# A planned kernel (Mamba block, experts, attention, MLP): other lengths and delays in the program that writes its instruction order

## The reference, cut to what matters

```python
xn = layernorm(x)
x = x + mamba_mlp_norm(xn) + experts(xn)              # layer 0
xn = layernorm(x)
x = x + attention_and_memory(xn) + lora_mlp(xn)       # layer 1

# mamba, per sequence: 512 channels, 16 states, a recurrence over 1024 tokens
h = exp(delta_t * A) * h + delta_t * B_t * u_t ;  y_t = sum over states of h * C_t
# then y * silu(res), output projection, MLP 256-1024-256 with exact gelu, a norm over the whole sequence
# experts, as written, come to a dense MLP 256-2048-256 on sequence 0, weighted per token
# layer 1: causal attention with 16 heads of 16 features, a memory gate built from 6-component lines,
# and an MLP 256-1024-256 whose weights get a rank-one-like correction per sequence
```

## Time and profile before

| what | us |
|---|---|
| median of the runs (3, from 3900.2 to 3905.79) | 3903.46 |
| the profiled execution, time on the device | 3907.57 |
| its span in the profile | 3905.8 |
| PE busy | 3610.2 |
| DVE busy | 3178.4 |
| ACT busy | 2659.1 |
| POOL busy | 2288.1 |

### The profile page before, as it was taken

How to read it: one execution, slowest core, us unless ns; L and a number is a source line. 1 busy time by engine, 2 the same in 40 slices (tenths; PEclk the granted TensorE clock), 3 DMA queues, 4 the chain that set the end, 5 groups by cost and what they waited for, 6 DMA issues and landing times.

```text
span 3905.8 us, 63544 instructions
## 1 busy us (share of the span) xinstructions
PE 3610.2 (92%) x20512; PEld 2387.7 (61%) x20512; DVE 3178.4 (81%) x6108; ACT 2659.1 (68%) x4049; POOL 2288.1 (59%) x1788
## 2 busy tenths in 40 slices
PE   7999999999999999999798999999999998999998
PEld 3666566655556565656565666666566666656665
DVE  3788999998999999998957687786868778686874
ACT  6877878787787878877534657566575656657565
POOL 4687898898999899999814142332414233241421
PEclk9999999999999999999897999999999999999999
DMA  4345444454544555554522123232322323232220
GB/s 155 126 155 162 154 156 157 161 165 151 163 161 153 159 164 171 162 166 144 184 74 90 52 58 97 72 100 67 99 65 69 93 68 104 67 94 64 73 80 26
DMA packets 253340, 456.88 MB, mean 117 GB/s; under 512 B 26116, under 2 KB 80852, under 8 KB 250196
## 3 DMA queue, kind: packets, MB, share of 16 engines
q1 hardware_dynamic: 253012, 452.82, 37.1%
HBM read 381.07 MB, written 69.21 MB: 115 GB/s over the span
## 4 chain that ended last, share of the span: by engine, by line
PE 46%; DVE 13%; ACT 9%; issue 8%; POOL 1%; DVEq 0%; ACTq 0%; POOLq 0%
PE ps L1495 6%; PE ps L1608 5%; PE ps L1600 5%; PE ps L1476 4%; PE ps L1458 3%; DVE ps L2013 3%; PE ps L1360 3%; PE ps L1410 2%; PE ps L1529 2%; PE ps L1370 2%; DVE ps L2036 2%; ACT L1625 2%; PE ps L1535 2%; ACT h L1625 2%; ACT exps L1625 2%
## 5 line engine op out<-in xcount | busy, mean ns | idle before, releaser
L2270 POOL TENSOR_TENSOR drive<-du,b_wide 128x1024 f32<-128x1024 f32 x512 | 1202.0, 2363 | 204.3 <-DVE held L2013 122.1
L2304 POOL TENSOR_SCALAR_AFFINE_SELECT exps<-exps 128x256 f32<-128x256 f32 x512 | 204.1, 413 | 1000.5 <-ACT exps L1625 1000.0
L1625 ACT ACTIVATE ps<-delta,neg_a 128x512 f32<-128x512 f32 x1024 | 681.7, 685 | 146.2 <-DVE heavy L1991 132.2
L1625 ACT ACTIVATE exps<-ps 128x1024 f32<-128x1024 f32 (+1 forms) x640 | 596.5, 938 | 255.2 <-PE ps L1476 249.2
L2036 DVE CUSTOM_DVE_ANT_0 ps<-ps,later 128x512 f32<-128x512 f32 (+3 forms) x1024 | 474.7, 518 | 90.6 <-PE ps L1458 88.6
L1410 PEld LDWEIGHTS ps<-p_all,heavy 128*128 128x128 f32 x3072 | 361.9, 144 | 246.5 <-DVE heavy L1991 124.8
L1410 PE MATMUL ps<-p_all,heavy 128*128 128x128 f32 x3072 | 439.9, 280 | 76.2 <-DVE heavy L1991 69.2
L1991 DVE TENSOR_TENSOR heavy<-c_wide,ps 128x512 f32<-128x512 f32 x704 | 467.6, 670 | 8.2 <-issue 4.1
L2013 DVE TENSOR_TENSOR_SCAN ps<-ps,carry,drive 128x512 f32<-128x512 f32 x352 | 441.5, 1272 | 32.8 <-ACT ps L1625 32.5
L2013 DVE TENSOR_TENSOR_SCAN ps<-ps,drive 128x512 f32<-128x512 f32 x352 | 420.4, 1214 | 48.3 <-ACT ps L1625 46.0
L2039 DVE TENSOR_REDUCE smax<-ps 128x2 f32<-128x1024 f32 x256 | 312.1, 1220 | 112.0 <-PE ps L1458 109.3
(11 more groups left out here) (211 smaller groups left out, 7158.7 us busy)
## 6 DMA issues: line engine op xcount, KB each, us to landing
b_wide<-bc_dram SPq DMA_DIRECT2D x512, 256.0 KB, 3.4
c_wide<-bc_dram SPq DMA_DIRECT2D x512, 256.0 KB, 3.5
stacks<-parts SPq DMA_DIRECT2D x192, 256.0 KB, 2.5
qs<-stacks SPq DMA_DIRECT2D x128, 192.0 KB
ks<-stacks SPq DMA_DIRECT2D x128, 192.0 KB, 4.3
x_row<-in_x SPq DMA_DIRECT2D x14, 1024.0 KB, 7.9
resid<-mix SPq DMA_DIRECT2D x9, 1024.0 KB, 5.3
x_row<-resid SPq DMA_DIRECT2D x9, 1024.0 KB, 5.4
```

What stands on the lines that cost most here:

```text
L1625: return nc.scalar.activation(out_, in_, func, **kw)
L2270: G.tensor_tensor(drive[:, g % DRIVE_SLOTS, :, :], du[:, e, :, :], wide(b_wide[:, g % B_SLOTS, :], MD), ALU.mult).then_inc(driven, 1)
```

## The change

It replaces the numbers in the planner's tables and adds three things to `by_time()`: a delay per producing engine (`LATE`) in place of 0.06 us for all, a delay between two dependent tasks of different kinds on the same engine (`OWN`), and an added 0.09 us from a scan to POOL. The share with which a PE task counts for the modelled clock is given per unit (`active_of`). `LEAD0`, `LEAD`, `LAG`, `SPANS`, `DRIFT`, `TURN`, `SHORT`, `RUN` and the ticks stay. One instruction of the fixed part moves: ACT's square root of the second part of sequence 0's layernorm now stands in the prelude, behind the drain of the second `xt` unit, and the first `norm` task is planned with 0.49 us in place of 3.2.

```diff
+LATE = {"p": 0.2, "a": 0.18, "v": 0.16, "g": 0.12, "s": 0.06}
+TO_POOL = 0.09
+OWN = {"p": 0.0, "a": 0.13, "v": 0.13, "g": 0.04}
-LENGTH0 = {"xt": 0.46, "xm": 1.74, "cv": 3.46, "res": 1.74, "xd": 3.46, "dl": 0.88, "yt": 0.46, "m": 3.46, "h": 1.74,
-           "o": 4.0, "mu": 0.4, "var": 0.4, "mh": 1.74, "mo": 3.5}
-EMPTY0 = {"xt": 0.66, "xm": 0.66, "cv": 0.66, "res": 0.66, "xd": 0.6, "dl": 0.68, "yt": 0.62, "m": 0.62, "h": 0.66,
-          "o": 0.42, "mu": 0.4, "var": 0.2, "mh": 0.62, "mo": 0.45}
+LENGTH0 = {"xt": 0.44, "xm": 1.72, "cv": 3.44, "res": 1.72, "xd": 3.46, "dl": 1.05, "yt": 0.44, "m": 3.46, "h": 1.72,
+           "o": 3.68, "mu": 0.2, "var": 0.2, "mh": 1.72, "mo": 3.46}
+EMPTY0 = {"xt": 0.48, "xm": 0.49, "cv": 0.58, "res": 0.49, "xd": 0.48, "dl": 0.59, "yt": 0.48, "m": 0.48, "h": 0.58,
+          "o": 0.33, "mu": 0.14, "var": 0.1, "mh": 0.49, "mo": 0.38}
...
-                add("v", ("scan", k), 1.2 if j % NC else 1.13, k, ("a", "decay", k), ("g", "drive", g),
+                add("v", ("scan", k), 1.175 if j % NC else 1.13, k, ("a", "decay", k), ("g", "drive", g),
...
-                    add("v", ("weigh", k), 0.6, k + 1.5, ("v", "scan", k), ("s", "c", g),
+                    add("v", ("weigh", k), 0.59, k + 1.5, ("v", "scan", k), ("s", "c", g),
...
-        add("v", ("gate", q), 1.66, at + NS * MD + 0.7, ("p", "add", piece_of(j, e + 1, 0, 0) - 1),
+        add("v", ("gate", q), 1.32, at + NS * MD + 0.7, ("p", "add", piece_of(j, e + 1, 0, 0) - 1),
...
-        add("a", ("norm", 0, t), 0.42 if t > TC else 3.2, t - TC - 2)
+        add("a", ("norm", 0, t), 0.49, t - TC - 2)
...
-            add("a", ("silu_x", j), 4.5, start + 2, ("a",) + unit)
+            add("a", ("silu_x", j), 4.4, start + 2, ("a",) + unit)
...
-            add("a", ("gelu", j), 6.2, start + 2, ("a",) + unit)
+            add("a", ("gelu", j), 6.1, start + 2, ("a",) + unit)
...
-LENGTH = {"xt": 0.44, "qk": 1.30, "pa": 1.18, "pb": 1.30, "lt": 0.44, "jw": 0.89, "fw": 0.44, "fr": 0.44, "ms": 0.44,
-          "zt": 0.44, "wo": 1.72, "e1": 0.23, "e2": 0.23, "f1": 1.30, "o": 3.44}
+LENGTH = {"xt": 0.44, "qk": 1.40, "pa": 1.28, "pb": 1.40, "lt": 0.44, "jw": 0.89, "fw": 0.44, "fr": 0.44, "ms": 0.44,
+          "zt": 0.44, "wo": 1.72, "e1": 0.23, "e2": 0.23, "f1": 1.46, "o": 3.44}
...
-    return 0.02 + sum(max(0.107, width_of(*one) / 2400) for one in unit)
+    return sum(max(0.12, width_of(*one) / 2230) for one in unit)
...
-WINDOW, LOW = 3.413, 0.45
-SHARES = {"sm": 0.5, "st": 0.5, "ms": 0.15, "e1": 0.03, "e2": 0.03, "mt": 0.25, "dl": 0.5}
+WINDOW, LOW = 3.413, 0.44
+ACTIVE0 = {"add": 1.2, "held": 1.2, "xt": 1.2, "yt": 1.2, "dl": 0.5, "mu": 0.0, "var": 0.0}
...
-        used[window] = used.get(window, 0.0) + part * share
+        used[window] = used.get(window, 0.0) + part * pace * active
...
                 for bank in banks[unit]:
-                    bank_free[bank] = end + 0.06
+                    bank_free[bank] = end + LATE[e]
...
-            felt = end + (late if one[0] != e or e == "s" else 0.0)
+            felt = end + (late if one[0] != e or e == "s" else OWN[e] if kind_of(one) != kind_of(name) else 0.0)
+            felt += TO_POOL if name[:2] == ("v", "scan") and one[0] == "g" else 0.0
...
                 elif kind == "norm":
-                    if (j, task[2]) == (0, TC):
-                        task_of(("root", 0, 1))
                     norm_tile(j, task[2])
...
                 if unit == ("cv", 0, MI - 1):
                     task_of(("silu_x", 0))
+                elif unit == ("xt", 0, 0, KD - 1):
+                    task_of(("root", 0, 1))
```

More of the change, by code:

```diff
@@ L219, in layer0_tasks, with add @@
     tasks, before = {}, {}
-    def add(engine, unit, length, tick, *after, late=0.06):
+    def add(engine, unit, length, tick, *after, late=None):
         kind = (engine, unit[0])
-        tasks[(engine,) + unit] = (length, tick, [a for a in after + (before.get(kind),) if a], late)
+        tasks[(engine,) + unit] = (length, tick, [a for a in after + (before.get(kind),) if a],
+                                    LATE[engine] if late is None else late)
         before[kind] = (engine,) + unit
@@ L502, in pair @@
             add("p", ("sm", g, n), scores_length(unit, max_width), tick, ("s", "stack", g) if n == 0 else None)
-            add("v", ("sm", g, n), sum(1.16 if it // TC > ch else 0.22 + max_width(it, ch) / 485 for it, ch in unit)
-                + (0.09 if n == len(MAX_UNITS) - 1 else 0), tick, ("p", "sm", g, n))
+            add("v", ("sm", g, n), sum(1.135 if it // TC > ch else 0.21 + max_width(it, ch) / 485 for it, ch in unit)
+                + (0.26 if n == len(MAX_UNITS) - 1 else 0), tick, ("p", "sm", g, n))
         place["mt", g] = first + TICKS - LEAD
@@ L554, in layer1_tasks @@
         for i in range(2):
-            add("s", ("rows", b, i), 3.8, start - 8, ("v", "split", b), ("p", "e2", b - 1, 3) if b else None,
+            add("s", ("rows", b, i), 3.3, start - 8, ("v", "split", b), ("p", "e2", b - 1, 3) if b else None,
                 late=3.0)
@@ L586, in layer1_tasks @@
             for ch in range(1, FCH):
-                add("g", ("sum", b, c, ch), 1.27, place["fr", b, c, ch] + 1, ("v", "fr", b, c, ch))
+                add("g", ("sum", b, c, ch), 1.22, place["fr", b, c, ch] + 1, ("v", "fr", b, c, ch))
             for i in range(2):
@@ L590, in layer1_tasks @@
             add("a", ("logistic", b, c), 0.5, place["ms", b, c, 1], ("v", "ms", b, c, 1))
-            add("v", ("gate", b, c), 2.9, place["ms", b, c, 1], ("a", "logistic", b, c), ("v", "pb", b, TC * c + TC - 1))
+            add("v", ("gate", b, c), 3.2, place["ms", b, c, 1], ("a", "logistic", b, c), ("v", "pb", b, TC * c + TC - 1))
         for kind in ("e1", "e2"):
@@ L612, in layer1_tasks @@
             dense(("wo", b, i), ("a", "zt", b, i // 2, KD - 1), v=[("v", "o", b, i, TQ - 1)])
-            add("s", ("store", b, i), 0.6, place["wo", b, i], ("v", "wo", b, i), late=3.0)
+            add("s", ("store", b, i), 0.5, place["wo", b, i], ("v", "wo", b, i), late=4.0)
     for g in range(PAIRS):
@@ L616, in layer1_tasks, with active_of, at_pace @@
     return tasks
-WINDOW, LOW = 3.413, 0.45
-SHARES = {"sm": 0.5, "st": 0.5, "ms": 0.15, "e1": 0.03, "e2": 0.03, "mt": 0.25, "dl": 0.5}
-def at_pace(used, start, length, share):
+WINDOW, LOW = 3.413, 0.44
+ACTIVE0 = {"add": 1.2, "held": 1.2, "xt": 1.2, "yt": 1.2, "dl": 0.5, "mu": 0.0, "var": 0.0}
+ACTIVE = {"xt": 1.2, "zt": 1.2, "lt": 1.1, "fw": 1.1, "fr": 1.1, "ot": 1.2, "mt": 1.2, "jw": 0.72, "ms": 0.24, "e1": 0.03, "e2": 0.03,
+          "pb": 0.62, "f1": 0.92}
+def active_of(unit, length):
+    if unit[0] != "L1":
+        return ACTIVE0.get(unit[0], 1.0)
+    if unit[1] in ("sm", "st"):
+        wide = places(MAX_UNITS[unit[3]], max_width) if unit[1] == "sm" else places(EXP_UNITS[unit[3]], exp_width)
+        return 1.1 * wide[1] / 2400 / length
+    if unit[1] == "pv":
+        return 2.56 * sum(exp_width(t, OUT_UNITS[unit[3]][1]) for t in OUT_UNITS[unit[3]][0]) / 2400 / length
+    return ACTIVE.get(unit[1], 1.0)
+def at_pace(used, start, length, active):
     now = start
@@ L703, in by_time @@
             mode = mode_of(unit)
-            end = at_pace(used, start, length, SHARES.get(unit[1] if unit[0] == "L1" else unit[0], 1.0))
+            end = at_pace(used, start, length, active_of(unit, length))
         del open_tasks[e][name]
```

96 lines of the change are left out of this document (49 added, 47 removed).

## The result

The changed kernel takes 3934.71 us (median of 4 runs, 3928.55 to 3936.72), the kernel before beside it 3903.88 (4 runs): **ratio 1.0077, 95% interval 1.006 to 1.0095**. It is 31 us slower, where 3883 was forecast with a range from 3845 to 3915. The profiled execution has a span of 3935.0 us. All lines of the program stand 25 lower in the file: L2013 is now L2038, L1458 is L1483, L1625 is L1650.

A forecast was written before the change was run, and what follows sets the result against it. It took PE as the bound to 330 us, DVE to 1962 and PE from 2140 to 3797. Terms of minus 9, 5, 0 and 6 made minus 20 us: 3883 us against a median of 3903.46, range 3845 to 3915.

The forecast's parts named there:

- The start, minus 9: Prelude: moving ACT's square root lets DVE and PE begin earlier, worth 9 us less.
- The 1.87 us of clock: Start: extra time of PE's next four matmuls at the lower clock, counted as gain beside 10.00 us of PE idle time.
- The lower of the two bounds: Start: DVE's own gain, its first scan at 58.5 instead of 61.30 us, 2.8 us; the upper end was 11.9 us.
- Lengths in layer 0, minus 5: Recurrence: more exact hand-off delays at 65 waits, 0.1 us each, taken as 5 us less; bounds minus 46 and plus 32.
- The hand-over, zero: The 178 us between layer 0 and layer 1: no change taken, bounds minus 10 and plus 10 us.
- Lengths in layer 1, minus 6: Layer 1: truer PE lengths and delays let other units fill part of PE's short waits, 6 us less.
- The bound on the bad side, plus 30: Layer 1: worst case for the term of minus 6 us, a good third of PE's 93.3 us idle time.
- The sign named for layer 1, a busy share of 94 to 95%: Layer 1: PE's busy share expected in the changed kernel's profile if the forecast holds.
- The other sign that it named, layer 1 alone moving by over 15 us: Layer 1: a move of over 15 us there would show the forecast to be wrong.
- (4): Slower: ACT's lumps in the recurrence come before decays and lose 32 to 48 us; 3926 us or more, chance 0.18.
- (2): Large gain, 45 to 65 us: half of DVE's 86 us of recurrence waits for ACT or POOL goes; 3851, chance 0.12.
- (3): No change: lists nearly alike, a small layer-1 loss takes back the start's 9 us; 3903 within 7.8 us, chance 0.15.

The follow-up runs named there:

- e1: The kernel before with only ACT's second square root moved into the prelude, all lists and banks unchanged: 3897.8 us, ratio 0.9985 to the kernel before.
- e2: The changed kernel, but with layer-1 task order and banks taken from the kernel before: 3894.6 us, ratio 0.9973 to the kernel before.
- e4: The changed kernel with the planner's modelled clock windows shifted by 1.7 us when layer 1's order is made: 3923.7 us, ratio 1.0056.
- e15: The changed kernel with layer 1's span `late` ending at 7 instead of 5 and modelled clock windows shifted by 1.7 us: 3890.5 us, ratio 0.9966.
- e3: Layer-0 order and banks of the kernel before, layer-1 order and banks of the changed kernel, square root moved: 3942.3 us, ratio 1.0106.
- e6: The changed kernel's layer 0; layer-1 lists from before's numbers with DVE drain `fr` at 0.76 instead of 0.75 us: 3934.4 us, ratio 1.0073.
- e5: The changed kernel's layer 0; layer-1 lists from before's numbers with modelled clock windows shifted by 1.7 us: 3932.5 us, ratio 1.0064.
- e11: The changed kernel with PE's old layer-1 lengths and LEAD, DRIFT, SHORT and span `mlp` reset, the planner's best of 320 settings: 3875.2 us, ratio 0.9923.
- e13: As e12, with the planner's modelled clock windows shifted by 1.7 us before the layer-1 lists are made: 3909.6 us, ratio 1.0014.
- e7: The changed kernel; layer-1 lists from the change's numbers with DVE drain `fr` at 0.68 instead of 0.67 us: 3931.1 us, ratio 1.0066.
- e14: As e12, with DVE drain `fr` planned at 0.68 instead of 0.67 us for the layer-1 lists: 3892.9 us, ratio 0.9961.
- e12: The changed kernel with layer 1's order made from the change's numbers but PE's lengths of before: 3884.6 us, ratio 0.9946.

## Why the prediction was wrong, by its own steps

**The start, minus 9.** The mechanism is right in its main steps: the root at 14.90 (forecast 14.9), DVE on at 15.13, the first scan at 59.32 (58.5). The size was too big. PE's idle time fell by 7.45 us, not 10, because ACT's drains of `delta` hold PE until 53.60 us, where the prediction has its list begin at 51.5. The 1.87 us of clock were hardly won back (3.55 against 3.75 us): the term assumed that a short gap leaves the clock up. It also read the clock wrong, which did not fall "while PE stood" but at 48.9 us, before PE stood; that gave 1.23 us at the end of the prelude which the term does not have. Alone the move is worth 4.8 us at 330 us and 5.9 (2.3 to 9.4) on the whole time (e1), and with the new lists of layer 0 only 1.9 are left at 330 us. The lower of the two bounds was nearer than I took it.

**Lengths in layer 0, minus 5.** With the start it was to be minus 14 at the last `gate`; it is minus 12.6. That agreement says little. The root alone gives 13.5 there, and 14 kernels with the very same lists of layer 0 (after, e2, e4 to e15) have that end between 1943.8 and 1956.0, mean 1949.4; the two with before's lists have 1948.0 and 1958.2. A term of 5 us can't be seen in this. It can be seen on the way: at the 512th scan, near 1030 us, the new lists are ahead of before's by 6.0 to 13.9 us, e1 and e3 with the root alone by 4.4 and 4.9. Little of the difference is left at the end of the layer.

**The hand-over, zero.** The cuts of 179 us above are of equal length because I set them so, and show nothing. Marks in the work do: counted from the last `gate`, the first score matmul starts at 38.0 us (before 46.6), the 48th matmul with the values at 120.3 (125.3) and the 384th, an eighth of them, at 350.3 (351.3). So zero is right to within a few us, and the loss lies behind these marks.

**Lengths in layer 1, minus 6.** This is the step that failed. It reads: "93.3 us of idle time at 0.51 us a wait are some 180 waits; if each gave 0.1 us, it would be 18 us. I take a third". It measured plus 42. The idle time was seen rightly as many short waits, and these did get shorter, by 16 us in the stretch. But the step treated a list as something that a better number improves a little everywhere. The list is rebuilt: another unit comes first, the rest follows, and 14 waits more than before are over 1 us. e2 and e3 put the whole loss on this list, and e6 shows that a change of no meaning costs as much. The bound on the bad side, plus 30, was worked out from idle time alone ("a good third of the idle time"). It left out that the instructions get longer too, which took as much again: 21 us idle and 21 us of longer instructions, with 75 us more at the lower level. The sign named for layer 1, a busy share of 94 to 95%, hides this: it was 93.4%, because the busy time grew as well. The other sign that it named, layer 1 alone moving by over 15 us, did show it.

**The rivals.** (4), slower, had the sign and nearly the time (3926 or more) but the wrong place: it put the loss in the recurrence, where waits for decays fell from 86.1 to 76.9 us. (2) fell: those waits were not halved. (3) said that ties depend on hundredths of a us, and used it only against "no change"; e6 shows that it is the main fact here. It should have widened the range: two redraws of before's own numbers lie 38 and 40 us above the list in place (e5, e6 against e2), and a range that ends at 3915 has no room for that. The chance of slower, 0.18, took the list in place for an average one.

**What stays open.** Which of the other numbers (delays, drains, DMA entries) alone helps or hurts in layer 1 was not tried one by one, and neither were order and banks. Why before's list was better than two redraws of it is not shown, though the planner's own model ranks it first. e11 was not redrawn, so it is a good list, not a proof of good numbers; e13 suggests that a redraw can cost 25 us.

## What to carry to other kernels

Where a program builds its order by playing numbers forward, any edit of a number draws a new list, right or not: here 0.01 us in one entry cost 1% of the time once (e6), and moved it by 0.1 and 0.2% in two other cases (e7, e14). So measure two or three trivial redraws before a change of numbers is judged, look first at the end that the model itself gives them, pick leads and spans again after it, and keep the fastest list by measurement.

To judge a list for a full PE by its profile, take the sum of all its idle time in the stretch. Over these 17 kernels the length of the stretch follows it with a correlation of 0.95 (a part of that is by construction, since the stretch is idle and busy time together), the number of gaps with 0.43, the sum of gaps over 1 us with 0.81 and the time at the lower level with 0.82. By the last two alone e5 (22 gaps in 39.3 us, 81.2 us at the lower level) and e12 (23 in 37.6, 81.6) are alike, and e5 is 48 us slower: its idle time is 115.8 us and e12's 90.7. The changed kernel had fewer waits than before and nearly the same busy share.

## What the hardware showed that I had not expected

- Idle time of PE in layer 1 comes with more than its own length. The gap before 3051.79 us (3.80 us idle) was followed by `f1` matmuls of 0.41 us against 0.28, and behind the last `gate` the 21 us of extra idle time came with 75 us more at the lower level and 21 us more busy time. Over the 17 kernels the stretch grows by 1.7 us for each us of idle time in it; that is a fit, and e5 against e2 has only 1.3 (14.9 us more idle time, 19.3 us longer, the same time at the lower level). At the start the four matmuls behind 2.55 us of idle time were nearly as slow as those behind 10.00 us (3.55 and 3.75 us). And the clock can fall without any such gap: before, it fell at 48.9 us while PE ran 64-row matmuls with 0.78 us of idle time in front of them.
- A table load of ACT is over when its row ends: 279 loads of 1283 ns on the page, and in 274 of them the next activation follows within 0.1 us, mostly 0.01, as at the start of the changed kernel; in the other five it waits for another engine or a DMA:

```profile
38.99 1.28 ACT L1650 ACT_TABLE_LOAD   x1
40.28 1.91 ACT L1650 ACTIVATE xm<-xm 128x2048 f32<-128x2048 f32 x1
```

  The drain of about 1.38 us which the Trainium skill, ScalarE: Activation LUTs, section "What ACT_TABLE_LOAD costs", adds to each load shows in no row here.
- Executions of one kernel spread more than the three of before let see: 18 of them in one job go from 3898.1 to 3917.2 us, so a difference of 0.15% (e1) needed 10 runs.
